# Expert tiles of 128 rows against pairs of 64-row blocks side by side in a two-layer mixture-of-experts kernel

## What is computed

```python
# one feed-forward part of a layer (hidden 256 in layer 0, 352 in layer 1)
xn = rms_norm(x, norm_scale)
scores = xn @ w_router.T                      # 8 experts
scores_topk, idx = top_k(scores, 2)
weights = softmax(scores_topk)
up = moe_linear(xf, ids, w_up)                # row i gets the weights of expert ids[i]
u, gate = split(up, 2)
h = u * silu(gate)
down = moe_linear(h, ids, w_down)
out = sum(down * weights) + skip
# attention of layer 0: gated, square of relu, within sequences of 256
# attention of layer 1: linear attention with a cumulated sum, 16 heads
```

## Time and profile before

| | |
|---|---|
| median of 3 runs | 747.86 us (741.56 to 764.09) |
| profiled execution | 741.62 us |
| its span, first to last instruction | 739.9 us |
| granted TensorE clock, mean | 0.941 |
| TensorE busy | 620.9 us, 84% |
| TensorE weight loads busy | 567.5 us, 77% |
| VectorE busy | 456.0 us, 62% |
| ScalarE busy | 264.9 us, 36% |
| GpSimd busy | 281.8 us, 38% |
| DMA | 133.59 MB, 181 GB/s in the mean |

### The profile page before, as it was taken

The page is one execution under the profiler, slowest core; times in us unless marked ns, Lnnn a source line. Parts: engine busy times, 40 slices in busy tenths (PEclk is TensorE's granted clock), DMA queues, the critical chain, the costliest instruction groups (busy, mean ns, idle before and its releaser), DMA issues.

```text
span 739.9 us, 15773 instructions
## 1 busy us (share of the span) xinstructions
PE 620.9 (84%) x4590; PEld 567.5 (77%) x4590; DVE 456.0 (62%) x1649; ACT 264.9 (36%) x549; POOL 281.8 (38%) x327
## 2 busy tenths in 40 slices
PE   1688798987969888778888987989979979988977
PEld 1377778777768787777877987978868968877966
DVE  7765545827448257455445664967967969763445
ACT  2134342532514324333323344326326326323221
POOL 2444552160440613563514446044245147052314
PEclk9999999999998999989899999979969989999989
DMA  7388786645545457757656885645645645657752
GB/s 257 102 242 277 220 248 181 181 125 163 163 126 157 125 166 207 229 171 231 204 155 192 246 246 162 170 135 153 189 137 142 196 123 163 203 156 230 236 138 74
DMA packets 113271, 133.59 MB, mean 181 GB/s; under 512 B 10931, under 2 KB 76227, under 8 KB 112806
## 3 DMA queue, kind: packets, MB, share of 16 engines
q1 hardware_dynamic: 104998, 115.79, 53.9%
q0 software_dynamic: 8192, 16.79, 7.6%
HBM read 103.83 MB, written 28.71 MB: 179 GB/s over the span
## 4 chain that ended last, share of the span: by engine, by line
PE 50%; DVE 26%; issue 9%; DMA 6%; another core or an unknown queue 3%; ACT 3%; POOL 2%; POOLq 0%; DVEq 0%; SPq 0%
PE up_gate L1052 13%; PE up_gate L1045 10%; PE y L1006 8%; DVE hidden L698 4%; DVE x_res L745 3%; DMA rows_dram<-rms_out,rows_of 2%; PE side L1067 2%; PE y L1008 2%; PE side L1133 2%; DMA y_rows<-y_dram,rows_of 2%; PE side L1149 2%; PE side L1083 1%; DVE root_square L725 1%; DVE root_square L724 1%
## 5 line engine op out<-in xcount | busy, mean ns | idle before, releaser
L698 DVE TENSOR_TENSOR hidden<-up_gate,hidden 128x256 f32<-128x256 f32 (+1 forms) x240 | 115.5, 489 | 193.7 <-ACT hidden L593 79.1
L504 POOL DMA_INDIRECT rows_dram<-rms_out,rows_of x128 | 129.8, 1014 | 249.7 <-DVE rows_of L855 183.2
L1052 PE MATMUL up_gate<-rows_T,up 128*128 128x128 f32 x1440 | 196.6, 287 | 21.0 <-ACT rows_T L598 8.7
L1052 PEld LDWEIGHTS up_gate<-rows_T,up 128*128 128x128 f32 x1440 | 182.1, 200 | 30.0 <-issue 15.6
L525 POOL DMA_INDIRECT y_rows<-y_dram,rows_of x120 | 121.0, 1008 | 183.5 <-issue 119.3
L593 ACT ACTIVATE hidden<-up_gate 128x256 f32<-128x256 f32 (+1 forms) x240 | 103.9, 436 | 240.8 <-PE up_gate L1045 112.8
L1045 PE MATMUL up_gate<-rows_T,up 128*128 128x128 f32 x960 | 139.5, 291 | 13.4 <-issue 9.0
L1045 PEld LDWEIGHTS up_gate<-rows_T,up 128*128 128x128 f32 x960 | 126.4, 203 | 24.1 <-issue 22.1
L1006 PE MATMUL y<-down,hidden 128*128 x480 | 77.9, 287 | 16.7 <-DVE hidden L698 14.8
L1006 PEld LDWEIGHTS y<-down,hidden 128*128 128x128 f32 x480 | 67.1, 202 | 18.4 <-issue 18.4
L1006 PE MATMUL y<-down_a,hidden 128*128 x480 | 75.9, 282 | 0.0
(11 more groups left out here) (195 smaller groups left out, 698.3 us busy)
## 6 DMA issues: line engine op xcount, KB each, us to landing
up<-in_up SPq DMA_DIRECT2D x120, 352.0 KB
up<-in_up SPq DMA_DIRECT2D x120, 256.0 KB
rows<-rows_dram SPq DMA_DIRECT2D x47, 256.0 KB
y_dram<-y_tile SPq DMA_DIRECT2D x45, 256.0 KB
rows_dram<-zeros SPq DMA_DIRECT2D x12, 256.0 KB, 3.3
rows<-rows_dram SPq DMA_DIRECT2D x16, 192.0 KB
y_dram<-y_tile SPq DMA_DIRECT2D x15, 192.0 KB
rows_dram<-rms_out,rows_of POOLq DMA_INDIRECT x128
```

Of the source, the lines that this page charges most:

```text
L504: pool.indirect_dma_start(out=xg_d[g], out_offset=bass.IndirectOffsetOnAxis(ap=pos[g][:, at:at + 1], axis=0), in_=xs(Z, GROUPS[g][c // TB] ...
L698: dve.tensor_tensor(h, u, h, ALU.mult).then_inc(mult_done, 1)
L1052: last = pe.matmul(U[q % 3][:, c * P:(c + 1) * P], upW[n % RING][:, at + c * P:at + (c + 1) * P], rows_, start=True, stop=True)
```

## The change

Expert rows are now padded to blocks of 64. At most 15 blocks result beside one fixed block for each expert: the first 64 rows of an expert go to its fixed block (rows from `FIXED_ROW` on), the others to free blocks in order of expert. A tile is a pair of blocks. In the first 8 tiles of a phase (`PAIRS`) the first half is free block a, whose expert is read from `eid`, and the second half is the fixed block of expert a, whose weights stand at a known place. The next three tiles (`FETCHED`) hold two free blocks each, the last one a single one: 12 tiles a phase, 192 in all.

`up` holds 64 rows stationary and moves the weights, 2 x 256 columns at once in layer 0, gate and up of 352 columns each in layer 1. The first half writes partitions 0 to 63 of the bank, the second 64 to 127, so the result has rows on partitions. As down needs hidden units on partitions, a new step `turn(t - 1)` transposes `hid` into a bank `H`, and ScalarE copies it to `hidT` (`copy_T`). `down(t - 2)` then multiplies 64 columns of `hidT` for each half. `y` has one bank instead of two; `H` takes the other.

All up weights are resident (`upR`). Only the second half of the three pairs of free blocks has its weights fetched, three fetches a phase in two or three DMAs each. Loads of rows and stores of y are two DMAs a round. `copy_T` is new on ScalarE; `assign` has two more VectorE operations; the counting row and the one-hots of the first round are prepared otherwise. The schedule tables have an entry for each batch and other offsets, and the last phase keeps eight early tiles and four late ones.

```diff
-PAD = 32
-RING = 6
-AHEAD = 4
+HALF = P // 2
 HEADS, F, G = 16, 4, 8
...
+BLOCKS = (2 * NT - 1) // HALF
+FIXED = E * HALF
+FIXED_ROW = BLOCKS * HALF
+PAIRS = E
+FETCHED = (BLOCKS - PAIRS) // 2
+TILES = [PAIRS + (BLOCKS - PAIRS + 1) // 2 for g in GROUPS]
 CH = [TB * len(g) for g in GROUPS]
...
-GATHER = 3
-STORE = 3
+GATHER = 2
+STORE = 2
 DOWN = 2
+TURN = 1
 ROWS_AT = 2
-LOAD_ROWS = 3
-LEAD = 38
-LAG = (3, 25, 9, 15, 2)
-
-COMBINE = (((8, 10),),
-           ((11, 16),),
-           ((7, 13),),
-           ((7, 10),))
-ATTENTION = (({3: 11, 4: 11, 5: 12, 6: 12, 7: 14, 8: 15, 9: 16, 10: 17, 11: 18, 12: 19, 13: 19, 14: 20, 15: 21},),
+LOAD_ROWS = 6
+FETCH = 2
+LEAD = 30
+LAG = (0, 0, 0, 0, 0)
...
-FIRST_SLOT = -30
+FIRST_SLOT = -60
...
-LATE = 8
+LATE = PAIRS
...
+LATE_MATRIX = [LATE_AT - LATE + at for at in (1, 4, 7, 10)]
+LATE_SUM = {SLOTS + DOWN: tuple(range(LATE_TILES))}
...
-        upW = [sb(f"up{i}", 2 * HIDDEN[1] + PAD) for i in range(RING)]
+        upR = [sb(f"up{l}", E * 2 * HIDDEN[l]) for l in range(2)]
+        upF = [sb(f"up_fetched{i}", 2 * HIDDEN[1]) for i in range(FETCHED)]
+        dnF = [sb(f"down_fetched{i}", 2 * P) for i in range(FETCHED)]
+        dnFb = [sb(f"down_b_fetched{i}", P, rows=96) for i in range(FETCHED)]
...
+            sp.dma_start(upR[0][:, :], up0).then_inc(up_loaded[0], 16)
...
-                sp.dma_start(tiles(xg[r % 4][:, 0:n * P]), xg_d[g][a * P:(a + n) * P, :].rearrange("(t p) d -> p t d", p=P)).then_inc(rows_loaded[r % 4], 16)
-
-            def load_up(n):
-
-                s, g = PHASE[n]
+                for dst, src in halves(xg[r % 4], xg_d[g], a, n, P):
+                    sp.dma_start(tiles(dst), src).then_inc(rows_loaded[r % 4], 16)
...
+            def halves(sbuf, dram, a, n, rows):
+
+                def rows_of(first, step):
+                    return dram[first:first + step * n, :].rearrange("(t p) d -> p t d", p=step)
+
+                if a < PAIRS:
+                    return ((sbuf[0:HALF, 0:n * P], rows_of(a * HALF, HALF)),
+                            (sbuf[HALF:P, 0:n * P], rows_of(FIXED_ROW + a * HALF, HALF)))
+                first = PAIRS * HALF + (a - PAIRS) * P
+                last = first + (n - 1) * P
+                return ((sbuf[:, 0:(n - 1) * P], dram[first:last, :].rearrange("(t p) d -> p t d", p=P)),
+                        (sbuf[0:rows, (n - 1) * P:n * P], dram[last:last + rows, :].rearrange("(t p) d -> p t d", p=rows)))
...
+            def fetch(s, g):
+
                 l = LAYER[s]
                 w = 2 * HIDDEN[l]
-                a = n - START[s][g]
-                if a == 0:
-                    sp.wait_ge(eid_ready, gidx(s, g))
-                if n >= RING:
-                    sp.wait_ge(gate_done, n - RING + 1)
-                    after(sp, up_done, n - RING + 1 - LAYER1)
-                v = sp.value_load(eid[g][0:1, a:a + 1], min_val=0, max_val=E - 1)
-                sp.dma_start(upW[n % RING][:, 0:w], (up0, up1)[l][:, bass.ds(v * w, w)]).then_inc(up_loaded[n % RING], 16)
+                k = PARTS.index((s, g))
+                sp.wait_ge(eid_ready, k + 1)
+                if k:
+                    sp.wait_ge(down_done, 3 * k)
+                for f in range(FETCHED):
+                    a = PAIRS + 2 * f + 1
+                    v = sp.value_load(eid[g][0:1, a:a + 1], min_val=0, max_val=E - 1)
+                    sp.dma_start(upF[f][:, 0:w], (up0, up1)[l][:, bass.ds(v * w, w)]).then_inc(fetched[f], 16)
+                    sp.dma_start(dnF[f][:, :], (down0, down1a)[l][:, bass.ds(v * (2 * P), 2 * P)]).then_inc(fetched[f], 16)
+                    if l:
...
+                for q in range(4):
+                    if t == 24 + 6 * q:
+                        w = 2 * HIDDEN[1] * E // 4
+                        sp.dma_start(upR[1][:, q * w:(q + 1) * w], up1[:, q * w:(q + 1) * w]).then_inc(up_loaded[1], 16)
...
-                    act.wait_ge(y_stored[r % 4], 16 * (r // 4))
-                act.activation(ysb[r % 4][:, 0:n * P], Y[r % 2][:, 0:n * P], ACT.Copy).then_inc(y_done, 1)
+                    act.wait_ge(y_stored[r % 4], 32 * (r // 4))
+                act.activation(ysb[r % 4][:, 0:n * P], Y[:, 0:n * P], ACT.Copy).then_inc(y_done, 1)
+
+            def copy_T(n):
+                w = CHUNKS[LAYER[PHASE[n][0]]] * P
+                act.wait_ge(hidT_done, n + 1)
+                act.activation(hidT[n % 3][:, 0:w], H[:, 0:w], ACT.Copy).then_inc(hidT_ready, 1)
...
-                        dve.memset(R[5], 1.0)
-                        link(dve.memset(R[4], 1.0))
-                        link(dve.tensor_tensor_scan(R[4], R[5], R[4], 0.0, ALU.mult, ALU.add))
...
-                    first_row = base[:, :].unsqueeze(1).to_broadcast([P, n, E])
-                    ro = tiles(row_of[:, 0:n * E], E)
-                    dve.scalar_tensor_tensor(ro, first_row, float(P), tiles(S[2][:, 0:n * E], E), ALU.mult, ALU.add).then_inc(s2_free, 1)
+                    ro, mv = tiles(row_of[:, 0:n * E], E), tiles(moved[:, 0:n * E], E)
+                    rank = tiles(S[2][:, 0:n * E], E)
+                    link(dve.scalar_tensor_tensor(to_free[:, :], base[:, :], float(HALF), fixed_end[:, :], ALU.mult, ALU.subtract))
+                    dve.scalar_tensor_tensor(mv, rank, float(HALF), to_free[:, :].unsqueeze(1).to_broadcast([P, n, E]), ALU.is_ge, ALU.mult)
+                    dve.tensor_tensor(ro, rank, fixed_row[:, :].unsqueeze(1).to_broadcast([P, n, E]), ALU.add).then_inc(s2_free, 1)
                     dve.wait_ge(s2_free, S2_TURN["rank", s1, b])
+                    link(dve.tensor_tensor(ro, ro, mv, ALU.add))
...
-                    last = dve.tensor_scalar(R[c], R[4], rows_1[:, 2 * c:2 * c + 1], None, ALU.is_equal)
-                link(last)
-                for c in range(TB):
-                    last = dve.scalar_tensor_tensor(R[c], R[4], rows_1[:, 2 * c + 1:2 * c + 2], R[c], ALU.is_equal, ALU.add)
-                last.then_inc(onehot_ready, 1)
+                    link(dve.tensor_scalar(R[c], R[4], rows_1[:, 2 * c:2 * c + 1], None, ALU.is_equal))
+                    dve.scalar_tensor_tensor(R[c], R[4], rows_1[:, 2 * c + 1:2 * c + 2], R[c], ALU.is_equal, ALU.add).then_inc(onehot_ready, 1)
...
+                at = n % 4 * P
+                a = n - START[s][g]
                 v = held.pop(n)
-                if a == 0:
-                    after(pe, y_done, r - 1)
+                if n % 4 == 0:
+                    after(pe, y_done, n // 4)
+                pe.wait_ge(hidT_ready, n + 1)
+                h = hidT[n % 3]
+                for c in range(CHUNKS[l]):
+                    k = P if c < 2 else 96
+                    for half in range(2 if a + 1 < TILES[g] else 1):
+                        if half == 0:
+                            w = (dn0, dn1a)[l][:, bass.ds(v * (2 * P) + c * P, P)] if c < 2 else dn1b[:, bass.ds(v * P, P)]
+                        elif a < PAIRS:
+                            w = (dn0, dn1a)[l][:, a * 2 * P + c * P:a * 2 * P + (c + 1) * P] if c < 2 else dn1b[:, a * P:(a + 1) * P]
+                        else:
+                            w = dnF[a - PAIRS][:, c * P:(c + 1) * P] if c < 2 else dnFb[a - PAIRS][:, :]
+                        last = pe.matmul(Y[half * HALF:(half + 1) * HALF, at:at + P], h[0:k, c * P + half * HALF:c * P + (half + 1) * HALF], w,
+                                         start=(c == 0), stop=(c == CHUNKS[l] - 1))
+                if n + 1 == END_ROUND[ROUND_OF[n]]:
+                    last.then_inc(down_done, 1)
+
+            def turn(n):
+
                 pe.wait_ge(mult_done, n + 1)
-                y = Y[r % 2][:, a * P:(a + 1) * P]
-                for c in range(2):
-                    w = (dn0, dn1a)[l][:, bass.ds(v * (2 * P) + c * P, P)]
-                    last = pe.matmul(y, hid[n % 4][:, c * P:(c + 1) * P], w, start=(c == 0), stop=(l == 0 and c == 1))
-                if l == 1:
-                    last = pe.matmul(y, hid[n % 4][0:96, 2 * P:3 * P], dn1b[:, bass.ds(v * P, P)], start=False, stop=True)
-                if n + 1 == END_ROUND[r]:
-                    last.then_inc(down_done, 1)
+                after(pe, hidT_ready, n)
+                for c in range(CHUNKS[LAYER[PHASE[n][0]]]):
+                    last = pe.transpose(H[:, c * P:(c + 1) * P], hid[n % 4][:, c * P:(c + 1) * P], ident[:, :])
+                last.then_inc(hidT_done, 1)
...
+                if PAIRS <= a < PAIRS + FETCHED:
+                    k = PARTS.index((s, g))
+                    pe.wait_ge(fetched[a - PAIRS], 32 * (k + 1) + 16 * max(0, k + 1 - PARTS.index((2, STEP[2][0]))))
+                block = a if a < PAIRS else 2 * a - PAIRS
+                v = pe.value_load(eid[g][0:1, block:block + 1], min_val=0, max_val=E - 1)
                 held[n] = v
-                rows_ = xgT[r % 3][:, a % 4 * P:(a % 4 + 1) * P]
-                if l == 0:
-                    q = UP_BANK[n, "both"]
```

(27 more changed lines are left out.)

128 lines of the change are left out of this document (79 added, 49 removed), and 10 rows, old and new, of tables (ATTENTION, COMBINE).

## The result

The kernel after took 771.0 us (median of 4 runs, 767.7 to 774.1), the kernel before 748.3 on the same chip, 23 us less. The change makes the kernel slower. The prediction was 754 (690 to 850): the time lies in the range, but the likeliest case, within 2%, was wrong. The profiled execution took 771.8 for its 769.7 us of span.

A forecast was written before the change was run, and what follows sets the result against it. TensorE was taken to bound the kernel, with waits on short VectorE chains between slots. Start 28, slots 461, side work 134 - 5, remainder 110 and tail 23.7 summed to 752 us of span, 754 forecast (range 690 to 850).

The forecast's parts named there:

- the likeliest case: Whole kernel: time about as computed, within 2%, 735 to 765 us; chance 0.33.
- Up: Up matmuls per slot: three lengths a pair, 1.29 us in layer 0 (0.88 before); five, 1.48, in layer 1 (1.32).
- Down, turn, switches: Per slot in layers 0 and 1: down 0.44 and 0.66 us, turn 0.22 and 0.33, two mode switches 0.22.
- The slots together: TensorE's 190 slots up to the last early rows: 461 us against 392 before, 69 us more work.
- Other engines: ScalarE a net 62 us more from 192 copies less 48 silus; VectorE 23 us less from 48 fewer products.
- Start: Until the first expert matmul: 28 us instead of 34.5, since the first row matmul waits only for the first one-hot pair.
- Transfers: Removing 240 weight loads is worth nothing directly; the unknown queue's 24 us in the chain halve to 12.
- The remainder: TensorE's waits, exposed weight loads and half-clock time between first expert matmul and last early store: 110 us, 156 before.
- Tail: From the store of the last early rows to the end: 23.7 us, unchanged.
- the halves do run together: The forecast assumed array halves run at the same time; its rival, halves in turn, gave some 962 us, chance 0.13.
- the waits did not shrink: Rival, faster: longer slots swallow VectorE's chain and unknown stalls end, remainder 70, 714 us; chance 0.31.
- The coupling tightens: Rival, slower: turn needs VectorE's product a slot earlier; remainder 156, 800 us, or dear switches (0.27 us), 815; chance 0.23.

The follow-up runs named there:

- a_turnmm: The kernel after with the turn as pairs of half-array matmuls with the identity instead of full transposes: 806.5 us, beside 754.8 for after on the third chip.
- b_plain: The kernel before with plain transfers in place of GpSimd's indirect ones, on the second chip: 661.9 us, 0.955 of before.
- b_resident: The kernel before with up weights resident in SBUF and without the 240 loads of tiles' weights, third chip: 773.7 us beside 738.6 for before.
- the plain pair: The kernels after and before, each with plain transfers in place of GpSimd's indirect ones: 669.4 and 662.5 us on the fourth chip, 667.0 and 661.9 on the second.
- a_plain2: The kernel after with plain transfers in place of GpSimd's indirect ones, rerun on the fourth chip: 669.4 us, 0.900 of before.
- b_plain2: The kernel before with plain transfers in place of GpSimd's indirect ones, rerun on the fourth chip: 662.5 us, 0.892 of before.
- a_down3: The kernel after with down(t-3) in slot t instead of down(t-2), on the second chip: 698.4 us, 1.010 of before.
- a_same2: The kernel after, unedited, run again on the fourth chip: 769.5 us beside 753.8 for before, 1.037.

## Why the prediction was right or wrong

**Up.** Wrong, and the largest term. The prediction had instructions in the order A1, A2, B1, B2 and charged three lengths for a pair. The trace shows A1, B1, A2, B2 with 0.01 us between halves: two lengths. Up takes 148.15 - 147.24 = 0.91 us in layer 0 and 717.74 - 716.51 = 1.23 in layer 1, against 1.29 and 1.48. It had named 0.9 as what would show this error. The Trainium skill, TensorEngine Tiling (Array Packing), section Key Properties under Tiling Modes, has tiles work independently and in parallel: this trace agrees, 0.01 us between the halves.

**Down, turn, switches.** Right. A down of 0.44 and 0.65 us (a_turnmm, where no switch follows), transposes of 0.11 with one pause of 0.06 in between that was not in the sum, 0.10 us a switch (0.11 predicted). The rule of the same page of the Trainium skill, section Key Properties, is that a change of mode drains the engine; the 0.10 us at each switch agree with it.

**The slots together.** 96 x 1.82 + 94 x 2.46 = 406 us, not 461. The change adds 14 us to before's 392, not 69.

**Other engines.** ScalarE rose by 40 us, not 62: the sum forgot that with 48 rounds for 64 the copies of rows and of y become fewer too (33.0 us in after for 42.3 in b_plain, 28.7 for 36.5: 17 us). VectorE fell by 26 (23 predicted). Neither mattered.

**Start.** Wrong: 36.4 instead of 28 us. The first gather by matmul did not wait for the first one-hot pair but for VectorE's copy of the second batch's scores, queued behind all of them. The sum priced the removed wait and did not ask what is late next.

**Transfers.** Wrong in sign. Their direct worth was put at nothing and the unknown queue's 24 us were halved, on the guess that dense transfers cause it. b_resident shows that taking the loads out of before costs 35 us (some 20 at least) on a chip with late completions, and the unknown releaser of after grew to 68 us.

**The remainder.** Wrong, and it covers up the error in the slots. From the first up to the last early store it is 746.9 - 36.4 = 710.5 us; less 406 and 129 it leaves 175, where 110 was predicted and before had 156. In the plain pair on the fourth chip it is 637.4 - 33.9 - 392 - 134 = 78 in before and 645.2 - 36.6 - 406 - 129 = 74 in after (store of the last early rows less first up, slots and side work). So its shrinking with the slots, 132 to 98 in the prediction, hardly happens: 78 to 74. The rest of the 156 and of the 175, 78 and 101 us, goes with the indirect transfers and their late completions. Part of it is the clock: TensorE's busy time is 620.9 - 592.0 = 29 us longer in before than in its plain form, and 620.9 - 582.3 = 39 in after. The stores that end these stretches, in after, a_plain2 and b_plain2 (count: shortest, median and longest in ns, start of the first to start of the last):

```profile
L470 SPq DMA_DIRECT2D y_early<-y_tile x4: 574/610/1199, 733.8 to 746.9; - x4
```

```profile
L470 SPq DMA_DIRECT2D y_early<-y_tile x4: 574/631/1243, 634.2 to 645.2; - x4
```

```profile
L421 SPq DMA_DIRECT2D y_early<-y_tile x2: 382/382/382, 629.0 to 637.4; - x2
```

**Tail.** 22.8 us for 23.7.

**The range.** By the prediction's own terms a remainder of 156 with dear switches is 754 + 46 + 61 = 861 us, not 850. The measured time is far from either.

The sum with measured terms: 36.4 + 406 + 129 + 175 + 22.8 = 769 us. Against the prediction's 752 that is 8 more at the start, 55 less in the slots, 65 more in the remainder. Without indirect transfers the change costs 7 us, close to the 6 that were predicted (754 for 748), but that is luck. The working gives 752 - 739.9 = 12 us of span, and it comes near the plain pair's 663.2 - 659.9 = 3 only since errors of opposite sign meet: 55 us less in the slots, 42 more in the remainder, 9 more at the start, 4 less in the tail. The forecast of "within 2%" fails on the first chip (and on the fourth, 1.037) by what indirect transfers take more from after than from before: 23 - 7 = 16 us on the first by the medians (27 by the ratio of 1.046), (769.5 - 745.3) - 7 = 17 on the fourth; on the third, before scatters too much. That all of it is late completions, with the clock behind them, is argued: after with indirect transfers was not run on the chip without late completions; its nearest kin there, a_down3, is 1.0% over before, the cost of the plain pair.

Of the rivals, the halves do run together, and the waits did not shrink. "The coupling tightens" had the right sign, a remainder that does not fall, and the wrong mechanism: VectorE's product is not what is late (1.6 us of waiting before the turn in after), TensorE's own completions are. What stays open is what makes TensorE's completions late, and how much of the 47 us of late time more in after comes of longer runs on GpSimd and how much of the hand-over that each slot has more.

## What to carry to other kernels

Ask what an unknown releaser in the chain coincides with before you shrink it: the change took away transfers that kept GpSimd's indirect transfers apart, and added one more hand-over from TensorE per slot, to a kernel whose hand-overs from TensorE are what such transfers delay. Price a tile by clean slots in the timeline and not by the total; a_turnmm's total agreed with the wrong theory. And when the same kernel takes 696 us on one chip and 754 on another, compare only within a chip, and run the unedited kernel in each group.

## What the runs showed of the hardware

- In three of the four groups of runs TensorE's semaphores rose up to 8 us after the recorded end of the matmul, 87 to 148 times a run, and only while GpSimd issued indirect transfers, which fill 33% of the span of after, or up to 1.9 us behind, 54% together; on the second chip never, with the same transfers. In the same stretches rises of all three engines are missing from the record. Plain transfers of the same 64 KB set off none (a_plain2, fourth chip). The Trainium skill, SBUF — State Buffer, section SBUF: two separate sides, says that a transfer cannot be slowed by an engine's work nor the reverse; no run here shows a conflict at a port, and what delays the completions is open.
- An indirect transfer holds GpSimd for 1.00 to 1.01 us in the mean of the scatters and of the gathers, a plain one for 0.55, and before is 31 us faster with plain ones even where no completion is late.
- Two half-array f32 matmuls with their own columns and their own half of the bank run at the same time: the pair costs one, 0.01 us aside. Switching between the half and the full array costs 0.10 us.
- The granted clock was 0.97 in the mean in the plain pair, where TensorE is busy for 88 and 90% of the span, and 0.92 in after, where it is busy for 81%. The same matmuls took 582.3 us of TensorE's time in a_plain2 and 619.1 in a_same2 on the same chip.
